# Weights of the next stage split ahead in one shared SBUF buffer, and the end of the front stage moved into self-attention's first round

## What is computed

```python
x = x + xattn(layernorm(x), ctx, mask, Wq, Wkv, Wo, bo)      # 16 heads of 64; q = x@Wq; k,v = ctx@Wkv; out@Wo + bo
x = x + attn(layernorm(x), ...)                              # 16 heads
x = x + ffn(layernorm(x), ...)

# attn
nq, ckv = rms(x @ w_cq, g_qnorm), rms(x @ w_ckv, g_kvnorm)   # 96 and 32 columns
gate = softmax((x @ w_gate).mean(axis=1))
k_rope = rope((x @ w_krope) / 16)                            # shared by the heads
out = g0 * attend(q(nq), k1(ckv, k_rope), v(ckv)) + g1 * attend(q, k(sel), v(sel)) + g2 * attend(q, k(x), v(x))
return out @ w_proj
```

## Time and profile before

| | before |
|---|---|
| time, median of 3 runs | 3541.45 us (3529.15 to 3542.26) |
| time of the profiled execution | 3545.98 us |
| span of the profiled execution | 3544.2 us |
| mean granted TensorE clock | 0.969 of full |
| PE busy | 3312.9 us (93%) |
| DVE, POOL, ACT busy | 1815.3, 1628.8, 1482.1 us |

### The profile page before, as it was taken

How to read it: one execution, slowest core, us unless ns; L and a number is a source line. 1 busy time by engine, 2 the same in 40 slices (tenths; PEclk the granted TensorE clock), 3 DMA queues, 4 the chain that set the end, 5 groups by cost and what they waited for, 6 DMA issues and landing times. The chain is left out here.

```text
span 3544.2 us, 52758 instructions
## 1 busy us (share of the span) xinstructions
PE 3312.9 (93%) x19140; PEld 2842.0 (80%) x19140; DVE 1815.3 (51%) x2937; ACT 1482.1 (42%) x2749; POOL 1628.8 (46%) x1118
## 2 busy tenths in 40 slices
PE   6999999999999999999999996889999787799997
PEld 4888888888888888888888885767767565678897
DVE  4454554555555455455555556575674634532213
ACT  3455555555555555555555542153453405221000
POOL 4454555455555455455555544041441316246573
PEclk9999999999999999999999998899999989899998
DMA  5211110111111111011101105100000120124221
GB/s 198 72 38 36 45 45 25 46 45 45 38 34 46 36 45 42 29 45 46 44 28 44 38 2 148 37 27 26 2 3 1 52 74 1 47 68 124 78 85 37
DMA packets 116365, 170.32 MB, mean 48 GB/s; under 512 B 12144, under 2 KB 89328, under 8 KB 107376
## 3 DMA queue, kind: packets, MB, share of 16 engines
q1 hardware_dynamic: 113264, 158.23, 14.2%
q0 software_dynamic: 2816, 8.46, 0.7%
HBM read 143.52 MB, written 23.13 MB: 47 GB/s over the span
## 5 line engine op out<-in xcount | busy, mean ns | idle before, releaser
L427 POOL TENSOR_TENSOR es<-es,e 128x512 f32<-128x512 f32 x480 | 622.7, 1297 | 966.1 <-ACT e L493 965.8
L489 ACT ACTIVATE e_hl<-sc 128x512 fp32r<-128x512 f32 x512 | 323.7, 632 | 738.7 <-DVE sc L557 738.4
L585 PE MATMUL ps_p<-c_hi,wkv_lo 128*128 128x512 f32 x1024 | 402.9, 393 | 4.6 <-PEq L115 4.6
L585 PE MATMUL ps_p<-c_lo,wkv_hi 128*128 128x512 f32 x1024 | 402.5, 393 | 0.0
L585 PE MATMUL ps_p<-wkv_lo,c_hi 128*128 128x512 f32 x1024 | 401.6, 392 | 0.0
L585 PE MATMUL ps_p<-wkv_hi,c_lo 128*128 128x512 f32 x1024 | 401.5, 392 | 0.0
L515 DVE TENSOR_TENSOR k_lo<-ps_p,k_hi 128x512 fp32r<-128x512 f32 x256 | 175.7, 686 | 440.6 <-ACT k_hi L455 440.6
L585 PE MATMUL ps_p<-c_hi,wkv_hi 128*128 128x512 f32 x1024 | 399.4, 390 | 0.0
L585 PE MATMUL ps_p<-wkv_hi,c_hi 128*128 128x512 f32 x1024 | 398.3, 389 | 0.0
L515 DVE TENSOR_TENSOR v_hl<-ps_p,v_hl 128x512 fp32r<-128x512 f32 x256 | 177.1, 692 | 429.4 <-ACT v_hl L455 428.4
L557 DVE TENSOR_SCALAR sc<-ps_s,topi 128x512 f32<-128x512 f32 x512 | 379.7, 742 | 0.3 <-PE ps_s L635 0.2
(11 more groups left out here) (401 smaller groups left out, 7083.7 us busy)
## 6 DMA issues: line engine op xcount, KB each, us to landing
raw<-in_ctx_t SPq DMA_DIRECT2D x64, 1024.0 KB, 4.9
dense_raw<-in_L_ffn_W_experts SPq DMA_DIRECT2D x64, 256.0 KB, 2.9
raw<-in_L_xattn_Wkv SPq DMA_DIRECT2D x4, 1024.0 KB, 4.8
q_hi_scratch<-qa_qh SPq DMA_DIRECT2D x16, 256.0 KB, 2.5
q_lo_scratch<-qa_ql SPq DMA_DIRECT2D x16, 256.0 KB, 3.4
q_hi<-q_hi_scratch SPq DMA_DIRECT2D x32, 128.0 KB, 5.0
q_lo<-q_lo_scratch SPq DMA_DIRECT2D x32, 128.0 KB, 4.7
o_t_scratch<-o_sb SPq DMA_DIRECT2D x32, 128.0 KB, 2.3
```

Source lines behind the costliest of these rows:

```text
L427: g.tensor_tensor(ES[:, GL], ES[:, GL], e, ALU.add).then_inc(summed, 1)
L489: a.activation(E2[:, s % 2, :, 0, :], sc, ACT.Exp, scale=DH ** -0.5).then_inc(exp_hi, 1)
L585: mm = t.matmul(ps_p[:, par % 2, :], lhs, rhs, start=m == 0, stop=m == 3 * KC - 1)
```

## The change

SBUF is laid out anew. One tensor `wa` of two times 4096 words a partition at the low end of SBUF holds weights (high and low parts) for the whole program; `xt_hi`, `xt_lo` and `raw` also live throughout. In the cross stages the weights of K and V are kept by half of the heads: half 0 in `wa`, half 1 in `xt_hi` and `xt_lo`. Each row block of Wkv is loaded by two DMAs of half the size and split by two instructions instead of one. In detail, by stage:

1. `stage_cross`, last batch: Wo is loaded into `raw` at step 48 and split into `wa` at steps 50, 53, 56 and 59 (ACT copy, POOL subtraction, 1024 columns each); the first two tiles of attention output are loaded at step 58.
2. `stage_front` begins without loading or splitting Wo. The low part of its first tile is made by DVE instead of POOL. Near its end ACT rounds the weights of the first attention round, and DVE subtracts two of their three parts.
3. Lines 832 to 866 are gone from `stage_front`; their work stands in the first round of `stage_attend`: PE starts with the mean and `keys` of tiles 0 to 3 (`AHEAD = 4`), then the 16 transposes; DVE does the chain of the ranks, the third part of the weights, and the shared keys ahead of its first tile; ACT instead of DVE copies the ranks. In the tile loop `keys` run four tiles ahead, so tiles 4 to 7 have none left.
4. `stage_attend`, last round: w_proj is loaded and split where a next round's weights would be.
5. `stage_project` begins without its weight. It loads the two small feed-forward weights and Wq behind its own loads; ACT rounds the two small ones in its fifth step and POOL subtracts. `stage_ffn_attend` begins with its first weights ready, and splits Wq at once.

The diff, cut to its core:

```diff
@@ stage_queries
+            if n < 2 + KC:
+                return [(WKV[hf][0][:, n - 2], WKV[hf][1][:, n - 2], raw(n)[:, hf * INNER:(hf + 1) * INNER]) for hf in range(2)]
-                    sp.dma_start(raw(n), wkv[(n - 2) * P:(n - 1) * P, :]).then_inc(raw_in[n % 2], 16)
+                    for hf in range(2):
+                        sp.dma_start(raw(n)[:, hf * INNER:(hf + 1) * INNER].rearrange("p (v f) -> p v f", v=2), rows[:, :, hf, :]
+                                     ).then_inc(raw_in[n % 2], 16)
@@ stage_cross
+        WO_AT = {50: 0, 53: 1, 56: 2, 59: 3}
+        WO_LOAD, OT_LOAD, HALF_DONE = 48, 58, 27
+                    if last and s == WO_LOAD:
+                        sp.wait_ge(clo_done, KC * (B * SLB - 2))
+                        for j in range(4):
+                            sp.dma_start(quarter(WO_raw, j)...).then_inc(wo_in[j], 16)
+                    if last and s in WO_AT:
+                        a.wait_ge(wo_in[j], 16)
+                        a.copy(quarter(WO_hi, j), quarter(WO_raw, j)).then_inc(wo_hi, 1)
@@ stage_front
-            for j in range(4):
-                a.wait_ge(wo_in[j], 16)
-                a.copy(flat(WO_hi[:, 2 * j:2 * j + 2]), flat(WO_raw[:, 2 * j:2 * j + 2])).then_inc(wo_split_hi, 1)
+                if k == B - 1:
+                    a.wait_ge(prefetched, 16 * len(prefetch))
+                    a.wait_ge(xo_done, B)
+                    for c0, c1 in PARTS:
+                        a.copy(WA[0][:, :, c0:c1], RAW[:, :, c0:c1]).then_inc(round_hi, 1)
@@ stage_attend
+            def copy_ranks():
+                for n, (dst, w, turned) in enumerate(((NQT, QL, nq_turned), (CKT, KVL, ck_turned))):
+                    a.wait_ge(turned, 1)
+                    a.copy(dst, ps[0:w, (6 - 2 * n) * 512:(8 - 2 * n) * 512]).then_inc(nqt_copied, 1)
             v.wait_ge(const_in, 48)
+            shared_keys_and_gates()
+            normalise_ranks()
+            v.tensor_tensor(W_lo[:, :, c0:c1], RAW[:, :, c0:c1], W_hi[:, :, c0:c1].bitcast(F32), ALU.subtract).then_inc(first_lo, 1)
+            rope_shared()
             def body(g, first, last):
+                if first:
+                    means()
+                    for b in range(AHEAD):
+                        keys(g, b)
+                    turn_ranks()
                 for b in range(B):
-                    if first or b >= LAGB:
+                    if first and b + AHEAD < B:
+                        keys(g, b + AHEAD)
+                    if not first and b >= LAGB:
                         keys(g, b)
@@ stage_project
-            a.wait_ge(w_in, 16)
-            a.copy(flat(W_hi[:]), flat(W_raw[:])).then_inc(w_hi_done, 1)
+                if k == HB:
+                    a.wait_ge(wc_in, 32)
+                    a.copy(flat(WC_hi[:]), flat(WC_raw[:])).then_inc(wc_hi_done, 1)
+            g.tensor_tensor(flat(WC_lo[:]), flat(WC_raw[:]), flat(WC_hi[:]).bitcast(F32), ALU.subtract).then_inc(wc_lo_done, 1)
```

More of the change, by code:

```diff
@@ L187, in _ @@
         def _(g):
-            for n, (hi, lo) in enumerate(PIECES):
+            for n in range(NP):
                 g.wait_ge(hi_split, n + 1)
-                g.tensor_tensor(lo, raw(n), hi.bitcast(F32), ALU.subtract).then_inc(lo_split, 1)
+                for hi, lo, src in parts_of(n):
+                    last = g.tensor_tensor(lo, src, hi.bitcast(F32), ALU.subtract)
+                last.then_inc(lo_split, 1)
         @block.vector
@@ L216, in split @@
             def split(n):
-                a.wait_ge(raw_in[n % 2], 16 * (n // 2 + 1))
-                a.copy(PIECES[n][0], raw(n)).then_inc(hi_split, 1)
+                a.wait_ge(raw_in[n % 2], raw_value(n))
+                for hi, _, src in parts_of(n):
+                    last = a.copy(hi, src)
+                last.then_inc(hi_split, 1)
             def turned_hi(b):
@@ L303, in stage_cross @@
         totalled, rec_done = sem("totalled"), sem("rec_done")
+        wo_in = [sem(f"wo_in{j}") for j in range(4)]
+        wo_hi, wo_lo, ot_in = sem("wo_hi_done"), sem("wo_lo_done"), sem("ot_in")
         block = ctx.enter_context(nc.Block())
@@ L386, in body @@
                         queries(i + 1, 0)
+                    if last and s == WO_LOAD:
+                        sp.wait_ge(clo_done, KC * (B * SLB - 2))
+                        for j in range(4):
+                            sp.dma_start(quarter(WO_raw, j).rearrange("p (k f) -> p k f", k=2), wo.rearrange("(k p) n -> p k n", p=P)[:, 2 * j:2 * j + 2]
+                                         ).then_inc(wo_in[j], 16)
+                    if last and s == OT_LOAD:
+                        sp.wait_ge(o_out, 16 * 4 * 2)
+                        for b in range(2):
+                            sp.dma_start(OT[:, b], o_t[b].rearrange("c p t -> p c t")).then_inc(ot_in, 16)
                     for n in after(s, 6):
@@ L958, in stage_attend @@
         LAGB = 3
+        AHEAD = 4
         STEPS = range(B + LAGB)
@@ L1002, in body @@
             def body(g, first, last):
-                if not last:
-                    sp.wait_ge(w_lo_done, 3 * (g + 1))
+                if first:
+                    sp.wait_ge(first_lo, 1)
+                else:
+                    sp.wait_ge(w_lo_done, 3 * g)
+                if last:
+                    sp.dma_start(PROJ_RAW.rearrange("p (k n) -> p k n", k=KC), w_proj.rearrange("(k p) n -> p k n", p=P)).then_inc(pw_in, 16)
+                else:
                     load_w(g + 1)
@@ L1050, in body @@
                     a.copy(T4[:, b, K1_, :, 0:NOPE], heads(vb[:, 2 * GV:3 * GV], G4)).then_inc(vv_copied, 1)
-                if not last:
-                    split(g + 2)
+                if last:
+                    a.wait_ge(pw_in, 16)
+                    a.copy(PW_hi, PROJ_RAW).then_inc(pw_hi, 1)
+                else:
+                    split(g + 1)
                 for k in STEPS:
@@ L1078, in body @@
                 for b in range(B):
+                    if first and b == 4:
+                        gates()
                     v.wait_ge(q_done, B * g + b + 1)
@@ L1089, in body @@
                     v.tensor_tensor(x_[:, :, H_:], R[:, 0, :, H_:], R[:, 1, :, 0:H_], ALU.add).then_inc(roped, 1)
-                if not last:
-                    split(g + 2)
+                if last:
+                    v.wait_ge(pw_hi, 1)
+                    v.tensor_tensor(PW_lo, PROJ_RAW, PW_hi.bitcast(F32), ALU.subtract).then_inc(pw_lo, 1)
+                else:
+                    split(g + 1)
                 for k in STEPS:
@@ L2174, in program @@
-        stage_project(nc, x1, x2, w_proj, ident, ROWS, XT_hi, XT_lo)
-        clear_semaphores(nc)
-        DENSE_RAW = ctx.enter_context(nc.sbuf_tensor("dense_raw", [P, GP, 2 * D], F32))
-        first_pieces = [piece for q in range(GP) for piece in hidden_piece(dense[0], DENSE_RAW, q, q)]
-        stage_ffn_attend(nc, ffn, (ident, rope_t), ROWS, XT_hi, XT_lo, LG, first_pieces)
-        stage_dense(nc, x2, xs, bs, ms, dense, order, norm2, ROWS, XT_hi, XT_lo, META, LG, DENSE_RAW, out)
+        RAW = sb("raw", [P, 2, KC, BLK])
```

355 lines of the change are left out of this document (190 added, 165 removed).

## The result

The changed kernel took 3494.01 us, median of 4 runs (3490.97 to 3496.17), for 3539.53 before: ratio 0.9884, 95% interval 0.9867 to 0.9901. (The ratio is an estimate from all runs of a timing; the two medians of the first divided give 0.9871.) The forecast was 3507, a gain of 34.5 us. Measured it is 41 us by the first ratio, 39 by the second, and 45.5 and 40.3 by the medians, so 5 to 11 us more than the sum gave. The sign and the mechanism held. The stated range began at 3494, so the first timing lies in it by a hundredth of a us, which is luck; the second, 3499, lies well inside.

A forecast was written before the change was run, and what follows sets the result against it. PE, busy 93% of the span, was taken as the bound, with gains only from its idle time at stage joints. Terms 1.5 + 1.2 - 8.0 - 14.6 + 0.4 - 8.9 - 6.1 = -34.5 us took 3541.45 to 3507, range 3494 to 3522.

The forecast's parts named there:

- Queries, +1.5: Queries stage: Wkv blocks in two half DMAs land 0.8 us later, delaying ACT and PE; +1.5 us, bounds 0 and +3.
- End of the cross stage, +1.2: Cross stage's last batch, step 59: POOL's subtraction of Wo's last quarter delays DVE without projection cover; +1.2 us.
- Start of the front stage, -8.0: Front stage's start: ACT rounds the first tile at once, PE starts at about 2151.3 instead of 2159.33; -8.0 us.
- Front end and first round, -14.6: Front stage's end into first attention round: keys hide the ranks' chain, weights are ready; -14.6 us, bounds -10 and -17.
- The new wait of 4.1 us: First attention round: PE, through at 2303.2, waits 4.1 us for DVE, which ends the eighth tile at 2307.3.
- Last round, +0.4: Last attention round: ACT rounds 2048 columns partly ahead of PE's first transposes; +0.4 us, bounds 0 and 1.9.
- project, -8.9: Project stage: PE starts at 2799.8 instead of 2809.17, -9.3, less 0.4 for POOL's subtraction holding up DVE; -8.9 us.
- Feed-forward, -6.1: Feed-forward start: PE can start with the stage, at 2854.5 instead of 2860.56; -6.1 us.
- The wide range: Whole time: 3494 to 3522 us, from the forecast's own range, rivals 1 to 3 and half the scatter of earlier runs.
- rival 3: Project and feed-forward starts: shorter pauses leave PE at full clock, more gain than forecast; -42 us, 3499; chance 0.06.
- Rival 5: Cross stage: the steady step gets longer with operands in other buffers; 0.1 us a step gives 3558; chance 0.04.
- Rivals 1, 2 and 4: Joints give back more, 3516, 0.13; Wo late at cross steps, 3511, 0.05; weight waits move earlier, 3523, 0.04.

The follow-up runs named there:

- the two pairs: Profiles of the kernel before and the changed kernel: the first, then both again unaltered; timed again, the changed kernel took 3499.31 us for 3539.58, ratio 0.9889.
- the exchange inside the dense stage: Changed kernel with the dense stage's weights' high part and the hidden activations' low part exchanged in SBUF; 3498.06 us, ratio 0.9883.

## Why the prediction was right where it was, and what it missed

**What bounds.** Right: PE's idle time at the joints was what there was to gain.

**Queries, +1.5.** 2.7 and 0.4 in the two pairs, 3.7 at most in an experiment, 1.6 between the middles of all profiles with two DMAs and with one. The term stands, as the middle of a quantity that varies from one execution to the next. The first wait grew by 1.3 us, for the 0.8 of the sum.

**End of the cross stage, +1.2.** About right in size: undoing Wo gave back 1.1 at least in the scores, 1.4 against the first profile. The place was right too: POOL's subtraction at step 59 held DVE's e_hl by 0.87 us, and PE had no projection to fill the wait. *The rule of the Trainium skill ("SBUF — State Buffer", the two separate sides), that the later of the two engines blocks for the other's instruction, agrees with that row: DVE's operation finished only behind POOL's.*

**Start of the front stage, -8.0.** Measured 15.54 - 7.56 = 8.0. PE starts 2.4 us behind the stage's first issue, as forecast. The sum was right, since it was made from the new chain alone; it didn't say that half of it belongs to the attention output and not to Wo.

**Front end and first round, -14.6.** Measured -13.8 and -14.6. From the mean to the ring, where it repeats, the sum had 64.1 us and the traces have 64.6, for 78.9 before. The chain was hidden with 2.6 us to spare, for 2.4 in the sum: the tables had landed 5.2 us behind the mean (5.8 counted), and the transposes took 1.91 us (2.0). The new wait of 4.1 us for DVE's ropes was there, at 4.5, and the experiments on the order of keys show its cause.

**Last round, +0.4, and project, -8.9.** The gap shrank by 9.2 us. The stretch around it gained 10.3 and 14.4 us; what is above 9.2 is the softmax part, 77.2 and 73.1 us for 78.3 and 78.1, with the clock. Its scatter hides the +0.4.

**Feed-forward, -6.1.** The gap shrank by 5.96. The project stage gave up 0.4 of it in the first pair, as taken for POOL's subtraction, and nothing in the second (-6.5); the term is too small to be told in these traces.

**What failed** is one step: the sum put every stretch without an edit at zero, and its own range for the joints (3499 to 3515) was narrow for that reason. They gave -17.2 and -3.0 us. The first timing, 3494, lies below that range; the second, 3499.3, on its edge. The wide range has a slip besides: rival 3's 3499 less half the scatter of 13 us is 3492.5, not 3494. Rival 3 named the clock, but mainly for other places. In the first profile after, the clock stayed low at the starts of the front, project and feed-forward stages, as before (0.57, 0.51 and 0.50 in the same windows):

```profile
2154.76:2159.76 5.00, 5.00 (x12) 3.94 (x13) 0.00 (x0) 0.00 (x0) 2.64 (x2) 0.51 0.93 238
2238.59:2243.59 5.00, 5.00 (x30) 5.00 (x31) 0.00 (x0) 0.81 (x2) 0.00 (x0) 1.00 0.37 102
...
2776.98:2779.98 3.00, 3.00 (x8) 2.39 (x9) 1.28 (x3) 0.32 (x1) 0.00 (x0) 0.58 0.99 298
2822.83:2828.83 6.00, 6.00 (x15) 4.70 (x16) 4.06 (x4) 2.38 (x2) 1.27 (x2) 0.51 0.59 156
```

Only the second row, the start of attention, is at full clock now, and that was in the forecast. In other executions rival 3 did come true in part. In three of the nine profiles with a short gap ahead of the projection, the projection began at full clock, as here in the exchange inside the dense stage:

```profile
2770.25:2773.25 3.00, 3.00 (x13) 2.46 (x14) 1.41 (x3) 0.45 (x1) 0.00 (x0) 1.00 0.91 304
```

From there to the end of the stage these three took 41.2 us, the six others 42.7 to 43.5: 1.5 us. At the feed-forward's start it was low in all. The clock gave more in the last softmax part, by amounts that differ from one execution to the next. The dense stage gave 3.5 us, 2.3 of them by a pace that no experiment traced to its cause. Rival 5, a longer cross step, didn't occur: the scores as a whole ran over 2022.7 us for 2022.2, and all 1024 products of the form in the earlier trace rows took 279 to 283 ns:

```profile
L678 PE MATMUL ps_s<-q_hi,k_hi x1024: 279/283/283, 112.9 to 2135.7; 128*128 128x256 f32 x171
```

Rivals 1, 2 and 4 didn't occur either: no gap of the cross stage from step 50 on is ended by ACT, and the ranks were ready in time.

## What to carry to other kernels

Work that is moved across a stage boundary gains what is laid over it: with the cover taken away, the same move gave nothing on balance. It can also bring a new wait with it, here 5.2 us for tables that the next stage loads. Ask of every gap at a joint which of the things loaded there comes last once the first is gone: two of them stood behind one gap here, and the subtraction of one slowed that of the other. Before a difference in an untouched stage is explained, profile both kernels once more; here 7 of 10 us were a pause that one profile out of fourteen did not have, and the softmax part of one kernel differed by 4 us with the clock.

## What the runs showed of the hardware

- A gap put down to "issue" can be a plain wait for another engine: 4.52 us here, ended 0.10 us after DVE's last rope, and 2.18 once that rope came earlier.
- The same 480 matmuls of a softmax part took 73.05 us at a mean granted clock of 0.98 and 77.20 at 0.91, in two executions of one kernel.
- A DVE operation on two SBUF operands took 1.55 us for 0.68 while a POOL operation of 2.38 us was under way, and ended 0.55 us behind it. In the 14 profiles this operation met one of POOL's, also on two SBUF operands, over 400 times with POOL first and more than 0.13 us to go: it ended 0.55 us behind POOL's each time (0.546 to 0.556).
- The other way round POOL is held: its sum of exponentials took 1.80 us for 1.29 when DVE's operation had begun 0.04 us earlier.
- PE, never idle and at full clock, had 170 products in 20 us in four profiles of one program and its relocations, and 172 in ten profiles of another with the same instructions in that stage. Why stays open.
